# Step one of a top-p attention network: exponentials a body ahead in half rows, maxima over 208 columns

## The reference

```python
def top_p_attention(X, W1, W2, W3):
    q = X @ W1.T @ W2.T;  k = X @ W3.T            # 64 wide
    probs = softmax(q @ k.T)                      # N x N
    keep = the largest of each row until they hold 0.9 of its mass
    A = probs * keep
    return A / A.sum(-1)

R = (adj + I) / row sums;  Xf = Xa = X;  Z = 0
for n in range(2):
    A = top_p_attention(Xa, W1, W2, W3)
    Xf = R @ Xf
    Xa = A @ Xa
    Z += Xf @ U1[n].T + Xa @ U2[n].T
return layernorm(x + layernorm(X + Z) * ln_g + ln_b)
```

## Time and profile before

| | |
|---|---|
| runs of the kernel, median | 1614.88 us (1613.98 to 1618.24, 3 runs) |
| the profiled execution, its own time | 1615.12 us |
| its span, first to last instruction | 1613.3 us |
| busy: DVE, PE, ACT, POOL | 1409.1, 1236.0, 895.8, 270.5 us |
| bodies 0 to 11 of step one | from about 75 to 486 us |
| step two | from about 487 us |

### The profile page before, as it was taken

The page is one execution under the profiler, slowest core; times in us unless marked ns, Lnnn a source line. Parts: engine busy times, 40 slices in busy tenths (PEclk is TensorE's granted clock), DMA queues, the critical chain, the costliest instruction groups (busy, mean ns, idle before and its releaser), DMA issues.

```text
span 1613.3 us, 29504 instructions
## 1 busy us (share of the span) xinstructions
PE 1236.0 (77%) x9162; PEld 1052.8 (65%) x9162; DVE 1409.1 (87%) x7395; ACT 895.8 (56%) x1685; POOL 270.5 (17%) x357
## 2 busy tenths in 40 slices
PE   8888888788888998797979794919681918457870
PEld 4666677566667897787878784718671817456870
DVE  5788888788885989998989899989998989989994
ACT  5667666777766556655555554525552524424535
POOL 0322213222220341314142210100010000000000
PEclk9989999999999998999989997959795968779885
DMA  5100000000003250413223230301130110203101
GB/s 181 44 2 1 2 1 2 2 1 2 1 2 116 103 199 21 161 44 128 68 103 91 82 138 34 128 1 61 69 128 1 64 65 28 101 1 128 44 2 42
DMA packets 16590, 96.42 MB, mean 60 GB/s; under 512 B 1251, under 2 KB 8930, under 8 KB 9730
## 3 DMA queue, kind: packets, MB, share of 16 engines
q1 hardware_dynamic: 16384, 94.14, 16.7%
HBM read 92.43 MB, written 1.70 MB: 58 GB/s over the span
## 4 chain that ended last, share of the span: by engine, by line
PE 45%; DVE 38%; ACT 9%; issue 6%; DVEq 1%; POOL 0%; DMA 0%; SPq 0%; ACTq 0%; POOLq 0%
PE bank L547 25%; PE bank L526 10%; DVE junkC L789 10%; DVE cand L746 9%; PE bank L487 7%; ACT E L621 4%; DVE E L1115 4%; PE bank L562 2%; DVE E L1117 2%; DVE sub L945 1%; DVE slots L844 1%; DVE junkS L789 1%; ACT S L621 1%; ACT H L712 1%; ACT blkT L648 1%
## 5 line engine op out<-in xcount | busy, mean ns | idle before, releaser
L648 ACT ACTIVATE blkT<-bank 128x512 f32<-128x512 f32 (+1 forms) x728 | 413.0, 568 | 468.2 <-PE bank L526 464.2
L547 PEld LDWEIGHTS bank<-X,blkT 128*128 128x128 f32 x2704 | 340.1, 197 | 149.8 <-issue 87.5
L547 PE MATMUL bank<-X,blkT 128*128 128x128 f32 (+1 forms) x2704 | 384.1, 286 | 64.7 <-ACT blkT L648 63.4
L746 DVE MAX8 cand<-E 128x8 f32<-128x32 f32 (+1 forms) x3172 | 413.7, 202 | 16.2 <-ACT E L598 15.4
L526 PE MATMUL bank<-ident,E 128*128 128x128 f32 x1144 | 189.1, 292 | 218.5 <-DVE E L1117 218.5
L789 DVE SCALAR_TENSOR_TENSOR junkC<-cand,st 128x208 f32<-128x208 f32 (+1 forms) x416 | 303.8, 768 | 3.7
L526 PEld LDWEIGHTS bank<-ident,E 128*128 128x128 f32 x1144 | 148.9, 153 | 221.6 <-DVE E L1117 220.2
L526 PE MATMUL bank<-ident,S 128*128 128x128 f32 x1560 | 239.9, 273 | 0.9 <-POOL S L408 0.9
L487 PE MATMUL bank<-kT,Q 64*128 64x512 f32 (+1 forms) x728 | 197.8, 618 | 7.8 <-ACT E L598 6.9
L547 PE MATMUL bank<-YA,blkT 128*128 128x128 f32 x1352 | 192.6, 287 | 8.4 <-ACT blkT L648 8.4
L598 ACT ACTIVATE E<-bank 128x512 f32<-128x512 f32 (+1 forms) x308 | 158.2, 567 | 64.6 <-PE bank L487 63.8
(11 more groups left out here) (203 smaller groups left out, 1263.3 us busy)
## 6 DMA issues: line engine op xcount, KB each, us to landing
S<-in_adj_dram SPq DMA_DIRECT2D x50, 1663.5 KB, 7.0
S<-in_adj_dram SPq DMA_DIRECT2D x2, 1455.6 KB, 8.7
X<-in_x_dram SPq DMA_DIRECT2D x6, 256.0 KB, 4.2
out_dram<-H SPq DMA_DIRECT2D x2, 768.0 KB
S<-in_adj_dram SPq DMA_DIRECT2D x2, 194.9 KB, 9.7
u_in<-in_L_gnn_U_dram SPq DMA_DIRECT2D x4, 64.0 KB, 9.7
w_in<-in_L_gnn_W_dram SPq DMA_DIRECT2D x2, 32.0 KB, 2.1
X<-in_x_dram SPq DMA_DIRECT2D x1, 64.0 KB
```

Source lines behind the costliest of these rows:

```text
L547: m = pe.matmul(bank[int(u.acc)][:, 0:width], blkT[:, slot, b * P:(b + 1) * P], rhs[:, j, 0:width], start=(j == 0), stop=(j == NT - 1))
L648: act.activation(blkT[:, slot, 0:w], BLK[early][slot][:, 0:w], ACT.Copy).then_inc(blk_done, 1)
L746: v.max(cand[:, par, xx, 8 * r:8 * r + 8], E[where_e[self.s, self.p]][:, xx, r * w:min((r + 1) * w, N)]).then_inc(s_max, 1)
```

## The change

The maxima of step one go over 208 columns: 16 runs for each tile instead of 26, so 32 instructions instead of 52 and 128 candidates for each row instead of 208. The runs no longer end with the chunks of logits, so their order is by the chunk in which each ends. `max_ready` is given when the last maximum is taken (`close`) and not behind the search. The exponentials of a pair are cut into five pieces: 0 takes the candidates of both tiles, 1 to 4 a half row each. Pieces 0 to 3 of pair p + 2 are put into body p, behind the evictions of its steps 8, 9, 11 and 13; piece 4 stands at the head of body p + 1. Body 0 keeps all of pair 1 at its head. The search adds the two half sums first, as step two does.

```diff
@@ -30,7 +30,7 @@
 
 
     LOG_RANGE = float(np.log(NP / DROP) + 0.1)
-    RUN = [P, P // 4]
+    RUN = [13 * P // 8, P // 4]
     NRUN = [NP // r for r in RUN]
     NC = [8 * n for n in NRUN]
     COARSE = [6, 7]
@@ -115,7 +115,7 @@
         add_unit(b, "R", 0, n)
     for c in range(NCH):
         b.emit[c] = (0, 1, c)
-    b.exps[1] = [(0, 0, 0)]
+    b.exps[1] = [(0, 0, k) for k in range(5)]
     for p in range(NPAIR):
         more = p + 2 < NPAIR
         b = new_body(True, 0, p, 0)
@@ -124,14 +124,18 @@
         if more:
             for c in range(NCH):
                 b.emit[c] = (0, p + 2, c)
+            for i, k in ((NCH + 1, 0), (NCH + 2, 1), (NCH + 4, 2), (NCH + 6, 3)):
+                b.exps[i] = [(0, p + 2, k)]
         elif p == NPAIR - 2:
             for c in range(EARLY[0]):
                 b.emit[2 + c] = (1, 0, c)
         else:
             for c in range(EARLY[0], EARLY[1]):
                 b.emit[NCH + c - EARLY[0]] = (1, 0, c)
-        if p + 1 < NPAIR:
-            b.first_exps = [(0, p + 1, 0)]
+        if p == 0:
+            b.first_exps = [(0, 1, k) for k in range(5)]
+        elif p + 1 < NPAIR:
+            b.first_exps = [(0, p + 1, 4)]
     b = new_body(False, 1, -1, 0)
     for n in range(TURN_R):
         add_unit(b, "R", 0, START_R + n)
@@ -626,17 +630,15 @@
                 e = E[where_e[s, p]]
                 if piece == 0:
                     act.wait_ge(max_ready, gp + 1)
-                if s == 0:
-                    for xx in range(2):
+
+                n = 1 if s == 0 else 2
+                if piece < n:
+                    for xx in ((0, 1) if s == 0 else (piece,)):
                         exp_candidates(gp, s, xx)
-                        ins = exp_rows(gp, e, xx, 0, N, 0)
-                    ins.then_inc(e_ready, 1)
-                elif piece < 2:
-                    exp_candidates(gp, s, piece)
                 else:
-                    xx, half = divmod(piece - 2, 2)
+                    xx, half = divmod(piece - n, 2)
                     ins = exp_rows(gp, e, xx, half * HALF[0], HALF[0] if half == 0 else N, half)
-                    if piece == 5:
+                    if piece == n + 3:
                         ins.then_inc(e_ready, 1)
 
             def empty_block(g, early):
@@ -730,9 +732,9 @@
                 def __init__(self, s, p):
                     self.s, self.p, self.n = s, p, 0
                     self.total = 2 * NRUN[s]
-                    per = BANK // RUN[s]
-                    self.order = [(c, xx, r) for c in range(NCH) for xx in range(2)
-                                  for r in range(c * per, min((c + 1) * per, NRUN[s]))]
+
+                    self.order = [((min((r + 1) * RUN[s], N) - 1) // BANK, xx, r) for r in range(NRUN[s]) for xx in range(2)]
+                    self.order.sort()
 
                 def step(self, count=1):
                     for _ in range(count):
@@ -746,9 +748,17 @@
                         v.max(cand[:, par, xx, 8 * r:8 * r + 8],
                               E[where_e[self.s, self.p]][:, xx, r * w:min((r + 1) * w, N)]).then_inc(s_max, 1)
                         self.n += 1
+                        if self.n == self.total:
+                            self.close()
 
                 def finish(self):
                     self.step(self.total - self.n)
+
+                def chunk(self, c):
+
+                    self.step(sum(1 for o in self.order if o[0] <= c) - self.n)
+
+                def close(self):
                     par = (self.s * NPAIR + self.p) % 2
                     dve.wait_ge(s_max, self.total)
                     top = cand[:, par, :, 0:NC[self.s]].rearrange("p x (n k) -> p x n k", k=8)[:, :, :, 0]
@@ -817,11 +827,8 @@
                 def scratch(xx):
                     return junkC[:, xx, 0:n]
 
-                if s:
-                    link(v.tensor_tensor(two(Z), Zh[:, par, :, 0], Zh[:, par, :, 1], ALU.add))
-                    z = two(Z)
-                else:
-                    z = Zh[:, par, :, 0]
+                link(v.tensor_tensor(two(Z), Zh[:, par, :, 0], Zh[:, par, :, 1], ALU.add))
+                z = two(Z)
                 link.post(v.tensor_scalar(two(DROPZ), z, DROP, None, ALU.mult))
                 link.post(v.tensor_scalar(two(LEAST), z, 1e-12, None, ALU.mult))
                 link(v.tensor_tensor(two(BUDGET), csum[:, par, :], z, ALU.subtract))
@@ -1065,7 +1072,7 @@
                     v.tensor_copy(Q[h0:h1, 2 * c:2 * c + m, :],
                                   q_ps[h0:h1, 0:w].rearrange("p (m x d) -> p m x d", x=2, d=P)[:, :, xx, :]).then_inc(kq_done, 1)
                 if c >= 2:
-                    runs.step(2 * BANK // RUN[0])
+                    runs.chunk(c - 2)
 
             for s in range(STEPS):
                 runs.finish()
```

## The result

The changed kernel takes 1554.3 us (1553.39 to 1555.54, 4 runs) where the kernel before takes 1614.43 beside it: a ratio of 0.9624, 95% interval 0.9607 to 0.9642. The prediction was 1554, the range 1544 to 1578. The profiled execution took 1554.54 us.

The account below looks back on a forecast made before the run. Both TensorE and VectorE were taken to wait once a body for ScalarE's block of exponentials; bodies fall from 34.3 to 29.0 us. Savings of 53.1 and 8.3, less 0.7, total 60.7: 1614.9 to 1554.2 us, range 1544 to 1578.

Parts of the forecast that it names:

- ten rounds, body 1 to body 11: Step one: one round at 28.4 us and nine at 29.0 make 289.4 where 343.0 were.
- cutting the blocks of pairs 0 and 1: ScalarE's exponentials for the first two pairs: one more start each, 0.35 us a time, costing 0.7 us.
- step two: The part after body 12: its own work is unchanged, so step one's saving should arrive undiminished.
- TensorE's path: Step one on TensorE: 6.2 us of stop and slow clock go, 0.3 to 0.5 of stalls come; 28.4 us a body.
- VectorE's path: Step one on VectorE: search 20.9 us plus settling 7.96, given as 28.8 us a body, bare links costing their wait.
- (b): Piece 0 on ScalarE waits for `max_ready`, 20.3 us against 19.4: a wait of 0.9 us, of which TensorE loses 0.6.
- (a): Late logits, chunk 6 stored 17.1 us into the body, delay VectorE's search: 28.1 us to the next `a_ready`, under 28.8.
- likeliest case: Step one: three loops at 28.8 to 29.6 us a body, 1552 to 1560 us; chance 0.55.
- TensorE alone bounds: Step one: bare waits cost nothing, VectorE's round is 27.1, a body 28.0 to 28.6 us, 1544 to 1551 us; chance 0.13.
- Body 11's head: Head without logits between: TensorE's stop goes too, 6.9 us and 1.4 of slow clock, 8.3 us saved.
- maxima waiting for stored logits: Sign in VectorE's search of step one that would show the prediction wrong; no size given.
- slower: A 208-column run holding eight kept weights sends its pair through `full`, at least 164 us more: 1718 or more; chance 0.04.

Follow-up runs that it names:

- the load on VectorE: Changed kernel plus three needless maxima over 128 candidates at the start of each search of step one, results unchanged: 1557.92 us, 29.01 us a body.
- the kernel with two maxima a link: Changed kernel with maxima over 128 columns, 52 of them, two behind each link of the search: 1591.62 us, 32.35 us a body.
- two halves together: Changed kernel with pieces 1 and 2, both halves of tile 0's row, together behind step 9's eviction, none behind step 11's: 1571.38 us.

## Why the prediction was right

**The mechanism** was as told: the block of exponentials at the head held both big engines and took TensorE's clock with it. The long stops are gone in bodies 1 to 10, one of 1.47 us is left in body 11, and the clock is 1.00 in all of them. The experiments add what the prediction only used: the move, the shorter search and the early `negm` need each other. The move with 128 columns brings 0, the width alone loses 10 us, both without the early `negm` lose 9, and all three bring 60.

**The sum**, term by term, from the profiled executions:

| term | predicted | measured |
|---|---|---|
| ten rounds, body 1 to body 11 | -53.6 | 343.0 to 285.9: -57.1 |
| start and body 0, to body 1's first turn | +0.5 | 108.9 to 110.6: +1.7 |
| body 11 to body 12's first turn | -8.3 | 34.6 to 28.1: -6.5 |
| cutting the blocks of pairs 0 and 1 | +0.7 | in the second row |
| step two | 0 | +1.4 |
| all | -60.7 | -60.5 |

So 1554.2 is closer than its parts deserve, and that is luck: an error of 3.5 us in the rounds met one of 3.7 us elsewhere. The 1.4 us of step two can't be told from nothing: from body 12's first turn on, where the work is the same, the kernels here take 1124.8 to 1131.4 us.

- *TensorE's path*, 28.4 predicted, 28.59 measured: the stalls around the half rows and the tile's end are a little longer than followed.
- *VectorE's path*, 28.8 predicted. The search was summed at 20.9 and took 20.77; the settling 7.81 instead of 7.96, because its second instruction no longer starts while GpSimd is at work (3.68 for 3.87 us). The prediction's own terms, 20.9 and 7.96, add up to 28.9 and not 28.8. With the 0.18 of waiting the round is 28.58, without it 28.4, as the load on VectorE confirms. That bare links cost their wait was right: in the changed kernel a small bare one still takes 0.19 to 0.20 us from start to start, and the kernel with two maxima a link came out at 24.43 for 24.6. The rule of the Trainium skill ("VectorE: DVE Perf Modes", The DRAIN you can't avoid), by which the round would be 27.1, isn't borne out by instructions of this size.
- *The handovers.* (b) was forecast as a wait of 0.9 us of which TensorE loses 0.6. The wait is 0.42, and by the load on VectorE it costs TensorE nothing, with 0.17 us to spare. This is the term of the sum that was too large. (a) was forecast at 28.1 us through chunk 6. Chunk 6 is stored at 156.48 and its first maximum starts at 156.95, so that loop has about 0.5 us to spare and 28.1 was right. The 0.18 that VectorE stands is for chunk 4 (the 19th maximum), which the prediction did not follow; the kernel with 256 columns shows such a wait (for chunk 5) where it binds. The loop that I missed, from `negm` over the half rows to the same pair's search, takes 11.0 us for its first part here, which ends 1.5 us before VectorE is free, so it did no harm to the number; in the kernels with a late `negm` it sets the time.
- *Which engine bounds.* I took 29.0, TensorE's path with what (b) would cost it; in fact it is TensorE's list alone at 28.59. That lies a hair under the band of my likeliest case and in that of "TensorE alone bounds", though not for its reason: bare waits are not free.
- *Body 11's head* was over-counted: it has no logits, so nothing covers piece 4 there, and TensorE stands for it:

```profile
399.59 1.13 PE L551 MATMUL bank<-X,blkT 128*128 128x128 f32 x8 [1.47 <-ACT blkT L650]
```

- *The start* varies: the first settling begins at 65.7 to 69.4 us in kernels whose start is the same, at 67.48 in the changed one's profile. How much of the 1.7 is the change's I can't say.

The sign "maxima waiting for stored logits", which was to speak against the prediction, does show, but with 0.18 us a body.

The rival "slower" through a run with eight kept weights did not occur: no instruction of `full` is in the profile.

## What to carry to other kernels

Where two engines both wait once a round for one block on a third, moving the block ahead pays only if what releases it comes ahead too: follow the loop from the releasing value to the work that makes the next such value, before the list is changed. A move that measures nothing by itself can be half of a large gain, so try it together with the part that shortens its release. When fillings hide waits, look at how long they last against when their own inputs arrive: here 26 left the engine standing and 52 came too late, while 32 did best.

## What the runs showed of the hardware

- Stops of TensorE of 1.47 us (body 11) and 1.72 us (two halves together, once a body) left its granted clock at 1.00; stops of 4.84 us and of 4.05 us (late `close`) were followed by the half rate, as in its row above where two products take 1.22 us for 0.60.
- GpSimd's two instructions on a tile's results took 0.46 and 0.29 us in the changed kernel's bodies 1 to 10, where before they took 3.5 to 3.9 us each when they started beside the settling, an instruction with two inputs from SBUF:

```profile
280.03 3.87 DVE L1117 SCALAR_TENSOR_TENSOR E<-E,st 128x3328 f32<-128x3328 f32 x1
...
276.64 3.78 POOL L437 TENSOR_TENSOR H<-hy,H 128x128 f32<-128x128 f32 x1 [15.97 <-ACT hy L684]
280.37 3.69 POOL L438 COPY YA<-hy 128x128 f32<-128x128 f32 x1
```

  VectorE's second instruction took 3.87 us where one of GpSimd's was still running at its start (the kernel before, 128 columns moved ahead, two halves together) and 3.68 where none was. The Trainium skill ("SBUF — State Buffer", SBUF: two separate sides) has such an instruction and a GpSimd one that reads SBUF shut each other out: whichever starts first holds the shared ports for its whole length. The rows agree, and the change moved them apart without meaning to. No engine waited for GpSimd's results either way; VectorE's 0.19 us a body was the cost.
